# A recommendation tower on one core: embeddings in a ring of two chunks, a fourth slot for split units, and unit D split in seven groups

## The reference

```python
e = jnp.stack([tbl_0[ids[:, 0]], ..., tbl_31[ids[:, 31]]], axis=1)     # 512 x 32 x 64
# layer i:
z = jnp.einsum('bhd,bfd->bhfd', hidden, x).reshape(B, hidden.shape[1] * F, D)
y = jax.nn.relu(jnp.einsum('bcd,oc->bod', z, w) + b[None, :, None])
# layer 0: hidden = first 64 rows of y, direct = the last 64; layer 1: direct = all 128 rows
z = concatenate(finals).sum(-1)                                        # 512 x 192
h = jnp.maximum(jnp.concatenate([z, dense_ctx], axis=1) @ W_top1 + b_top1, 0.0)
h = jnp.maximum(h @ W_top2 + b_top2, 0.0)
y = h @ W_top3
```

## Time and profile before

| | |
|---|---|
| time, median of 3 runs | 1091.94 us (1091.52 to 1092.54) |
| the profiled execution: its time | 1092.62 us |
| the profiled execution: its span in the trace | 1090.8 us |
| mean granted TensorE clock, share of full speed | 0.978 |
| busy in the span: TensorE | 1025.0 us (94%) |
| VectorE | 944.4 us (87%) |
| POOL | 915.5 us (84%) |
| ScalarE | 734.9 us (67%) |

### The profile page before, as it was taken

One profiled execution on the slowest core, in us unless ns is written; L12 is line 12 of the kernel. 1 busy time (PEld: TensorE's weight loads), 2 busy tenths in 40 slices (PEclk: granted clock), 3 DMA queues, 4 the chain that ended last, 5 costly groups with the idle time before them and its releaser, 6 DMA issues.

```text
span 1090.8 us, 10701 instructions
## 1 busy us (share of the span) xinstructions
PE 1025.0 (94%) x3493; PEld 651.4 (60%) x3493; DVE 944.4 (87%) x623; ACT 734.9 (67%) x907; POOL 915.5 (84%) x300
## 2 busy tenths in 40 slices
PE   2059999999999999999999999999999999999999
PEld 1025556656666666666666666666666666666664
DVE  4059999999999999999999999999998989888982
ACT  1036666767777677777777777777777777777761
POOL 7526878779999999999999899997989888988890
PEclk9569999999999999999999999999999999999999
DMA  4278777687878787778877878787777877786730
GB/s 137 55 188 200 194 186 184 180 198 190 210 178 205 183 213 187 192 191 199 207 185 192 201 181 208 182 206 194 194 184 194 204 183 187 191 208 184 183 84 1
DMA packets 142074, 196.89 MB, mean 180 GB/s; under 512 B 15858, under 2 KB 57458, under 8 KB 141891
## 3 DMA queue, kind: packets, MB, share of 16 engines
q1 hardware_dynamic: 137922, 192.01, 70.3%
q0 software_dynamic: 4096, 4.20, 1.8%
HBM read 175.18 MB, written 20.97 MB: 180 GB/s over the span
## 4 chain that ended last, share of the span: by engine, by line
PE 86%; DVE 4%; issue 4%; DMA 3%; ACT 2%; SPq 1%; DVEq 0%; ACTq 0%
PE py L610 40%; PE py L626 15%; PE py L616 14%; PE py L617 14%; DVE zf L498 2%; ACT zh L362 2%; PE py L631 1%; DMA xs<-x_dram 1%; DMA x_dram<-xf 1%; DMA xs<-in_L_rec_w 1%; PE pt L592 1%; DVE zl L515 1%; PE py L675 0%; PE pzS L675 0%; DVE zf L459 0%
## 5 line engine op out<-in xcount | busy, mean ns | idle before, releaser
L303 POOL TENSOR_TENSOR zl<-zf,zh 128x2048 fp32r<-128x2048 f32 x168 | 772.3, 4610 | 116.2 <-ACT zh L362 114.2
L498 DVE TENSOR_TENSOR zf<-xs,hid 128x2048 f32<-128x2048 f32 x256 | 583.3, 2283 | 67.1 <-ACT hid L377 51.9
L610 PE MATMUL py<-zf,wf 128*128 128x512 f32 x1072 | 485.2, 596 | 6.5 <-DVE zf L498 6.5
L362 ACT ACTIVATE zh<-zf 128x2048 fp32r<-128x2048 f32 x186 | 354.9, 1908 | 44.5 <-DVE zf L498 41.1
L610 PEld LDWEIGHTS py<-zf,wf 128*128 128x128 f32 x1072 | 203.5, 190 | 214.2 <-issue 194.2
L616 PE MATMUL py<-zh,wh 128*128 128x512 f32 x744 | 293.6, 395 | 8.7 <-ACT zh L362 8.7
L617 PE MATMUL py<-zh,wl 128*128 128x512 f32 x744 | 292.1, 393 | 0.0
L626 PE MATMUL py<-zl,wh 128*128 128x512 f32 x744 | 233.8, 436 | 0.0
L498 DVE TENSOR_TENSOR zf<-xs,px 128x2048 f32<-128x2048 f32 x64 | 146.4, 2288 | 37.8 <-DMA xs<-x_dram 35.9
L626 PEld LDWEIGHTS py<-zl,wh 128*128 128x128 f32 x744 | 135.9, 189 | 59.2 <-issue 29.2
L293 POOL DMA_INDIRECT emb<-in_tbl,idx x128 | 143.1, 1118 | 29.9 <-issue 24.5
(11 more groups left out here) (71 smaller groups left out, 439.8 us busy)
## 6 DMA issues: line engine op xcount, KB each, us to landing
xs<-x_dram SPq DMA_DIRECT2D x640, 256.0 KB
x_dram<-xf SPq DMA_DIRECT2D x64, 320.0 KB
emb<-in_tbl,idx POOLq DMA_INDIRECT x128
xs<-in_L_rec_w SPq DMA_DIRECT2D x2, 512.0 KB
xs<-in_L_rec_w SPq DMA_DIRECT2D x1, 1024.0 KB
wt<-in_W_top SPq DMA_DIRECT2D x1, 512.0 KB
wt1b<-in_W_top SPq DMA_DIRECT2D x1, 256.0 KB
wt1a<-in_W_top SPq DMA_DIRECT2D x1, 128.0 KB
```

The lines of the kernel that those rows point to most:

```text
L303: pool.tensor_tensor(zl[:, q], zf[:, s], zh[:, q].bitcast(F32), ALU.subtract).then_inc(lo["P"], 1)
L362: act.activation(zh[:, q], zf[:, s], ACT.Copy).then_inc(hi, 1)
L498: dve.tensor_tensor(zf[:, slot(u)], left, right, ALU.mult).then_inc(mult, 1)
L610: mm = pe.matmul(y, wf[:, w, h], zf[:, s, h], start=first and h == 0, stop=ends and h == T - 1)
```

## The change

Four things change. The embeddings become a ring of two chunks, so that a gather for chunk 2 or 3 waits until the chunk two before it has been staged, and the gathers are spread anew over groups 0 to 43. The rings `zh` and `zl` get a fourth slot. D gets split weights (one more high and one more low weight at set-up). And D is split in the groups from 43 on whose number is 1 modulo 3 (43, 46, 49, 52, 55, 58 and 61), its low part made on VectorE: its `high` goes on ScalarE between `finish_straight(g+1)` and `finish_dir1(g+1)`, its `low` on VectorE after `add_1(g+1)`, and its `late` on TensorE after late B(g) in the next group. Such a group is closed by D's late matmuls.

```diff
-ZF, ZS = 5, 3
+ZF, ZS = 5, 4
 def mode(unit):
     name, g = unit
+    if name == "D" and 43 <= g < LAST and g % 3 == 1:
+        return "V"
     if name in "PD":
         return "F"
...
-LATER_GATHERS = [(c, f) for c in range(1, NC) for f in range(F)]
+CHUNK_GATHERS = [[3] * 10 + [2] + [0] * 2, [3, 2, 2, 2, 2, 2, 2, 2, 2, 2, 2, 2, 2, 2, 3], [0] + [3, 2, 2, 2, 2, 2, 2, 2, 2, 2, 2, 2, 2, 2, 3]]
+CHUNK_GATHERS = [(c + 1, n) for c in range(NC - 1) for n in CHUNK_GATHERS[c]]
 def gathers(g):
-    first = min(3 * g, 33) + 2 * max(0, g - 11)
-    return LATER_GATHERS[first:first + (3 if g < 11 else 2)]
+    if g >= len(CHUNK_GATHERS):
+        return []
+    c, n = CHUNK_GATHERS[g]
+    first = sum(m for b, m in CHUNK_GATHERS[:g] if b == c)
+    return [(c, f) for f in range(first, first + n)]
...
-SPLIT_NAMES = "ACB"
+SPLIT_NAMES = "ACBD"
...
 def closing(g):
+    if mode(("D", g)) != "F":
+        return ("D", g)
...
-        emb = sb("emb", [P, F, NC, D])
+        emb = sb("emb", [P, F, 2, D])
...
             def gather(c, f):
+                if c >= 2 and f == 0:
+                    pool.wait_ge(staged, GC * (c - 1))
                 pool.indirect_dma_start(
-                    out=emb[:, f, c, :], out_offset=None, in_=tables[f],
+                    out=emb[:, f, c % 2, :], out_offset=None, in_=tables[f],
...
-                cols = emb[:].rearrange("p f c d -> p f (c d)")[:, :, ND * k:ND * k + ND]
-                act.activation(stage[:], cols, ACT.Copy).then_inc(staged, 1)
+                d = ND * (k % GC)
+                act.activation(stage[:], emb[:, :, k // GC % 2, d:d + ND], ACT.Copy).then_inc(staged, 1)
...
                 high(("B", g))
                 if g + 1 < G:
                     finish_straight(g + 1)
+                high(("D", g))
+                if g + 1 < G:
                     finish_dir1(g + 1)
                     finish_swapped(g + 1)
...
                 products(("A", g))
                 add_1(g)
+                if g >= 1:
+                    low(("D", g - 1))
                 if g + 1 < G:
                     products(("P", g + 1))
...
                 main(("A", g))
                 if g >= 1:
                     late(("B", g - 1))
+                    late(("D", g - 1))
                 if g + 1 < G:
                     main(("P", g + 1))
                     tail(g + 1)
```

More of the change, by code:

```diff
@@ L157, in dlrm_tower @@
         emb_flat = emb[:].rearrange("p f c d -> p (f c d)")
-        act1 = emb_flat[:, 1024:3072].rearrange("p (m n) -> p m n", m=4)
-        act2 = emb_flat[:, 3072:4096].rearrange("p (m n) -> p m n", m=2)
-        yrow = emb_flat[0:1, 4096:4608]
+        act1 = emb_flat[:, 0:2048].rearrange("p (m n) -> p m n", m=4)
+        act2 = emb_flat[:, 2048:3072].rearrange("p (m n) -> p m n", m=2)
+        yrow = emb_flat[0:1, 3072:3584]
         py1 = ps("py1", [P, N])
@@ L374, in finish_straight @@
                 else:
-                    act.wait_ge(w_low, 3)
+                    act.wait_ge(w_low, 4)
                 act.activation(hid[0:H, 0], py1[0:H], ACT.Relu, bias=bias0[0:H]).then_inc(straight, 1)
@@ L640, in _ @@
             pe.wait_ge(s_low, 3)
-            pe.wait_ge(w_low, 3)
+            pe.wait_ge(w_low, 4)
             turn_x(0)
```

## The result

The changed kernel takes 1109.7 us (median of 5 runs, 1108.58 to 1111.15) against 1092.54 of the kernel before, measured with it: a ratio of 1.0154, 95% interval 1.0142 to 1.0166, so 17.2 us slower. The profiled execution took 1109.36 us, its span is 1107.5, at a mean clock of 0.978 as before. The forecast was 1105.2, within 1099 to 1112.

A forecast was written before the change was run, and what follows sets the result against it. TensorE was taken to set the pace, with high A only 1.03 us in hand on ScalarE. 12.3 (ScalarE and TensorE) + 1.0 (group 43) = 13.3 on 1091.94 gave 1105.2 us, range 1099 to 1112.

The forecast's parts named there:

- ScalarE's run and late D: In six split groups, high D delays high A and main A, late D follows: main P 1.9 us later each.
- Group 61: Last split group: high A has 1.96 us in hand and is just in time, so only late D costs, 0.9.
- The exclusion of VectorE's and POOL's low parts: Low D waits for POOL's low part through shared SBUF ports: 1.0 us in group 43, bounds 0 and 2.2.
- VectorE's lateness: After low D, VectorE's 0.4 us beyond TensorE's lateness fits in its 1.50 us wait for straight: no cost.
- Gathers, ring, slots and set-up: Moved gathers are covered by POOL's waits, slots and set-up cost nothing: 0 taken, gathers uncovered at most 4 us.
- a low part is moreover only used after other units: Reason given that gathers delaying POOL's low parts would not reach TensorE; cost taken as 0.
- Sum: Whole kernel: 12.3 for ScalarE and TensorE plus 1.0 for group 43, 13.3 us slower.
- TensorE did not stay the bound: Rival: D's high part is covered and seven groups give back 0.69 us each, 1087.1 us; 7 in 100.
- The clock did not fall: Rival: the clock falls in TensorE's new gaps, 12 us more over seven groups, 1117 us; 4 in 100.
- VectorE was held for about half of one low part of POOL: Rival: low D locked out for a whole POOL low part, P 2.8 us late in six groups, 1122 us; 5 in 100.
- ScalarE's delay was not half hidden: Rival: high A's margin is 2 us or more in most groups, time within 2 us of 1091.9; 4 in 100.

The follow-up runs named there:

- e2: The changed kernel with D's low part not made and late D reading the high part again; ratio 1.0118 to the kernel before.
- e1: The changed kernel with D whole in every group; ring, gather spread, fourth slot and D's split weights stay; ratio 1.001 to the kernel before.
- e4: The changed kernel with D split only in groups 46, 49, 52, 55 and 58; ratio 1.0092 to the kernel before.
- e11: The changed kernel, D split only in groups 46 to 58, high A, copy_xf, late C, low D reordered, POOL's low A after low D; ratio 1.0017 to the kernel before.

## Why the prediction was right, and where its sizes were off

- *ScalarE's run and late D, 1.9 us in a steady group*: right, step by step; the split groups are 17.44 us long (17.4 said). The run grew by 1.85 (1.81 said), main A started 0.14 after high A (0.13 said), TensorE stood still 0.63 before main D and 1.49 before main A (0.8 and 1.5 said), late D and the slower first pair added 1.0. Measured 1.98. The idle copy shows the first half by itself, the single late matmul the second.
- *Group 61, 0.9*: 1.04.
- *The exclusion of VectorE's and POOL's low parts, taken at 1.0 in group 43 with bounds 0 and 2.2*: it is there. Low D(43) began at 763.26 (763.6 said) and was held until POOL was done. Group 43 and the one behind it lost 3.46, where 1.9 + 1.0 were said; 1.9 + 1.5 is what it came to, between the bounds. The mechanism was right, the term mis-sized by 0.5: of the 1.5, 0.6 came in group 43 itself, where the 1.0 had been put, and 0.9 behind it, by the lateness of main B(44), which only the upper bound had in it. That the exclusion goes both ways is what the Trainium skill, page "SBUF — State Buffer", section "SBUF: two separate sides", says of a VectorE instruction with two SBUF inputs and a GpSimd instruction that reads SBUF, and here the trace agrees: low D took 4.64 us against POOL, and POOL's low A 5.31 and 6.07 against low D.
- *VectorE's lateness "lies within the 1.50 us that it waits"*: this step failed at the end. It holds where two whole groups follow. Behind group 61 there is only one full group, VectorE's lag went through high C(62) to POOL's last three low parts, and TensorE lost 2.7 us that the sum did not have. e2, without low D, has none of it. Part of that lag was the exclusion, which the sum had looked at in groups 52 and 43 only: in group 61 it held low D for 1.64 us.
- *Gathers, ring, slots and set-up at 0*: right in sum, 1.001 in e1. But gathers do reach TensorE where POOL is late already, against "a low part is moreover only used after other units": 0.43 us in group 44 of e4, 0.79 in that of e11, and 0.4 to 1.2 in group 14 of every kernel with the ring. In the changed kernel's group 44, TensorE itself was late, and late A(44) found its low part ready.
- *Sum*: 13.3 said, 17.2 measured; of the difference of 3.9, 2.7 is the end, 0.5 group 43, some 0.4 the five steady groups. The rest, with the 0.4 that the first 44 groups came earlier in the profile, is within what profiles differ by. That the time lies in the range all the same is in part luck: its upper end had room for 4 us of gathers, which did not come, and the 2.7 of the end, of which the range knew nothing, fell into that room.
- *The rivals*: TensorE did not stay the bound. The clock did not fall: 1.00 from 850 to 900 us, with gaps of up to 1.5 us. VectorE was held for about half of one low part of POOL (2.4 us) in group 43 and for 1.64 us in group 61, and in the steady groups for 0.6 only. ScalarE's delay was not half hidden.

Not settled: why the load that copy_x0 waits for comes up to 1.3 us later in some executions than in others (0.68 us of waiting in e1, 1.64 in e4, 2.01 in e11, and 1.64 before).

## What to carry to other kernels

An engine that is busy a smaller share of the time has no time to give unless its idle time lies behind the work that others wait for; read from the rows when its result is ready and when it is used, and compare that margin (here 1.03 us) with what you want to insert (1.8) plus what you shorten beside it (1.6). When work moves off the bound onto two other engines, make the sum for each of them: here the second (VectorE) ate the gain as soon as the first (ScalarE) was out of the way. A lateness that later groups absorb in the steady part can come back at the end of the pipeline, where no group is left to absorb it.

## What the runs showed of the hardware

A subtraction on VectorE with both operands in SBUF (zf and zh) and one of the same kind on POOL overlapped by less than 0.2 us: whichever came second was held. VectorE's products, which read one operand from PSUM (hid or px), were not: products D(52) took their 2.28 us at 902.99 of the changed kernel, in the middle of POOL's low C and low B(52). Low D took 2.28 us alone and up to 4.64 when POOL was in a low part; POOL's 4.6 us became 5.31 and 6.07 when VectorE was in one, and a gather of 0.96 us became 2.83. The recorded duration of the held instruction includes the wait, so it shows as a longer instruction and not as idle time.
